# The delta stage's products with the inverses as 32x32 tiles in crossed row groups, its key products as tiles of 32 columns

## The reference, cut to what matters

```python
q = l2norm(silu(h @ Wq)); k = l2norm(silu(h @ Wk)); v = silu(h @ Wv)
beta = sigmoid(h @ Wb); alpha = exp(-exp(A_log) * softplus(h @ Wa + dt_bias))
def step(S, (q_t, k_t, v_t, a_t, b_t)):
    S = S * a_t
    delta = (v_t - k_t @ S) * b_t
    S = S + outer(k_t, delta)
    return S, q_t @ S * scale
o = rms_norm(o) * o_norm_w * silu(h @ Wg); out = o @ Wo
```

## Time and profile before

| | |
|---|---|
| Time, median of 3 runs | 2097.25 us (2090.12 to 2099.79) |
| The profiled execution | 2083.64 us, span 2081.6 us |
| PE busy | 1736.5 us (83%) |
| DVE, ACT, POOL busy | 1258.1, 1067.8, 873.5 us |
| Rows ahead of the loop | from about 1063 to 1148 us |
| 24 looped rows | 1148 to 1765 us, most 25.28 us apart |
| 8 rows of the tail | 1765 to 1975 us, most 26.3 to 26.5 us apart |

### The profile page before, as it was taken

The page is one execution under the profiler, slowest core; times in us unless marked ns, Lnnn a source line. Parts: engine busy times, 40 slices in busy tenths (PEclk is TensorE's granted clock), DMA queues, the critical chain, the costliest instruction groups (busy, mean ns, idle before and its releaser), DMA issues. The chain is left out here.

```text
span 2081.6 us, 37284 instructions
## 1 busy us (share of the span) xinstructions
PE 1736.5 (83%) x12051; PEld 1241.9 (60%) x12051; DVE 1258.1 (60%) x3243; ACT 1067.8 (51%) x3158; POOL 873.5 (42%) x1095
## 2 busy tenths in 40 slices
PE   0899629974299849999868999999999999899887
PEld 0344429864198826556557677777777777555533
DVE  7587624536345378787667566655665665456556
ACT  0443204331143328788544566656666666666643
POOL 0246646546555513343318756070606060622233
PEclk9997659995599959999979999999999999999999
DMA  2920023322122250000023221212121212110001
GB/s 63 416 69 22 30 72 107 97 85 84 49 70 63 58 195 23 26 25 25 25 77 80 60 57 47 57 47 57 47 58 46 57 48 60 53 48 29 25 12 41
DMA packets 155838, 135.89 MB, mean 65 GB/s; under 512 B 87957, under 2 KB 128214, under 8 KB 153494
## 3 DMA queue, kind: packets, MB, share of 16 engines
q1 hardware_dynamic: 146582, 115.08, 18.9%
q0 software_dynamic: 9088, 18.70, 2.8%
HBM read 77.17 MB, written 56.54 MB: 64 GB/s over the span
## 5 line engine op out<-in xcount | busy, mean ns | idle before, releaser
L2676 DVE TENSOR_TENSOR delta_sv<-delta_sv,delta_zp 32x256 f32<-32x256 f32 x384 | 161.2, 420 | 168.4 <-PE delta_zp L2317 162.0
L818 POOL DMA_INDIRECT y<-moe_y,moe_aim x156 | 177.1, 1135 | 161.4 <-DVE moe_y L958 69.0
L2589 POOL TENSOR_TENSOR delta_dd<-delta_ll,delta_minus 128x1024 f32<-128x1024 f32 (+1 forms) x9 | 24.3, 2700 | 382.4 <-DMA delta_ll<-lanes 382.3
L1771 ACT ACTIVATE field_p<-field_sp,field_nm 128x128 f32<-128x128 f32 x512 | 179.9, 408 | 0.9 <-DVE field_nm L1855 0.8
L2596 POOL TENSOR_TENSOR delta_dd<-delta_dd,delta_prod 128x30 f32<-128x30 f32 (+11 forms) x270 | 151.4, 561 | 21.1
L2594 POOL TENSOR_TENSOR delta_prod<-delta_ll,delta_dd 128x30 f32<-128x30 f32 (+11 forms) x270 | 139.4, 516 | 21.2
L2317 PE MATMUL delta_zp<-delta_sv,delta_ct 128*32 128x128 f32 x1536 | 122.5, 281 | 20.1 <-DVE delta_sv L2676 12.4
L2285 PE MATMUL delta_xp<-delta_la,delta_di 128*128 128x256 f32 x512 | 121.4, 392 | 12.9 <-DMA delta_di<-inverses 7.0
L1771 ACT ACTIVATION_READ_ACCUMULATOR field_p<-field_sp,field_nm 128x1 f32 x512 | 127.6, 249 | 0.0
L2317 PEld LDWEIGHTS delta_zp<-delta_sv,delta_ct 128*32 128x32 f32 x1536 | 70.3, 110 | 85.0 <-DVE delta_sv L2676 50.7
L2285 PEld LDWEIGHTS delta_xp<-delta_la,delta_di 128*128 128x128 f32 x512 | 97.3, 194 | 37.6 <-issue 25.3
(11 more groups left out here) (564 smaller groups left out, 4554.3 us busy)
## 6 DMA issues: line engine op xcount, KB each, us to landing
delta_al<-alpha SPq DMA_DIRECT2D x33, 512.0 KB, 4.4
pairs<-c_none SPq DMA_DIRECT2D x16, 1032.0 KB, 16.3
moe_xg<-pairs SPq DMA_DIRECT2D x78, 129.0 KB, 2.2
moe_yt<-y SPq DMA_DIRECT2D x16, 512.0 KB, 4.5
w_E<-in_E_dram SPq DMA_DIRECT2D x1, 4624.0 KB, 36.9
w_E<-in_E_dram SPq DMA_DIRECT2D x8, 578.0 KB, 4.0
lanes<-delta_la SPq DMA_DIRECT2D x128, 32.0 KB, 1.7
delta_di<-inverses SPq DMA_DIRECT2D x64, 64.0 KB, 2.3
```

The source lines that it names most:

```text
L818: nc.gpsimd.indirect_dma_start(results, bass.IndirectOffsetOnAxis(ap=aim[:, t % AR, j:j + 1], axis=0), y[:, t % YS, j, :], None).then_inc( ...
L1771: last = nc.scalar.activation(p[:, slot, h, :], s_ps[i][:, k, :], ACT.Exp, bias=nm[:, slot, h:h + 1], accum_out=zs[:, slot, h:h + 1])
L2676: nc.vector.tensor_tensor(sv[rows, two, :], sv[rows, two, :], z_ps[2 * pair // HH][rows, at, :], ALU.subtract).then_inc(s["z_kept"], 1)
```

## The change

The pairs of heads get numbers, 0 to 3, and CROSS = [0, 3, 1, 2]. For pair c the tokens' blocks of la lie crossed: block g of the keys is written to the 32 partitions g ^ CROSS[c] (^ is exclusive or) instead of g. What is per token on the partitions of la is crossed with it: eye, ball_at (a crossed copy of beta), and ck, for which a third product with headpick is made from a crossed copy of the norms' first 128 columns (four copies of 32 partitions each). squares for kn stay uncrossed.

key_products makes, for each head, four products with 32 columns of keys as weights, each over the tokens from its own block on (256, 192, 128 or 64 columns); the very first row's are over all 256. invert makes four products for each head: weights are a 32x32 inverse, read from the 32 partitions g ^ CROSS, written to the partitions g of x_ps, over the columns behind block g only. di shrinks to 32 columns and is not cleared any more. store_lanes issues 16 DMAs a row, one for each partition group and pair of heads. PE's wait for the placed inverses moves ahead of norms of the row before, and its wait for sq at the start of a looped step goes. In norms the two heads of a partition group are now 2g and 2g + 1.

```diff
+    CROSS, STORED = [0, 3, 1, 2], 16 * NB * PAIRS
+    def crossed(ap, pair):
+        part = CROSS[pair]
+        return bass.AP(ap.tensor, ap.offset + BL * part, [list(ap.ap[0]), [-2 * BL if part & 2 else 2 * BL, 2], [-BL if part & 1 else BL, 2], [1, BL]])
+    def by_blocks(ap):
+        return ap.rearrange("p (a b c) -> p a b c", a=2, b=2)
+    PRODUCTS = [(j + c, g ^ 3 * (j // 2)) for c in range(2) for g in (0, 1) for j in (0, 2)] + [(j + c, g ^ 3 * (j // 2)) for c in range(2) for g in (3, 2) for j in (0, 2)]
+    def lanes_of(part):
+        return slice(part * BL, (part + 1) * BL)
...
+        ball_at = m.sb("ball_at", [128, GROUPS + 1, GB * H])
...
-        di = m.sb("di", [128, 2, GB * H, T])
+        di = m.sb("di", [128, 2, GB * H, BL])
...
                 def store_lanes(p):
                     sp.wait_ge(s["la_kept"], p.n * 2 + 2)
-                    for g in range(NB):
-                        sp.dma_start(dram["lanes"][p.pair, g, p.b * H:(p.b + 1) * H, :, :].rearrange("h j i -> j h i"),
-                                     la[g * BL:(g + 1) * BL, p.slot, :, g * BL:(g + 1) * BL]).then_inc(lanes_out[p.half], 16)
+                    for part in range(NB):
+                        for pair in range(PAIRS):
+                            at, two = p.b * H + 2 * pair, slice(2 * pair, 2 * pair + 2)
+                            sp.dma_start(dram["lanes"][p.pair, part, at:at + 2, :, :].rearrange("h j i -> j h i"),
+                                         la[lanes_of(part), p.slot, two, lanes_of(part ^ CROSS[pair])]).then_inc(lanes_out[p.half], 16)
...
-                        sp.dma_start(di[g * BL:(g + 1) * BL, pair, two, g * BL:(g + 1) * BL],
+                        sp.dma_start(di[lanes_of(g), pair, two, :],
...
                         for g in range(4):
-                            last = nc.tensor.matmul(k_rows[g * 32:(g + 1) * 32, :], w["headrow"][:, a, :], sq[:, g + 4 * a, :],
+                            last = nc.tensor.matmul(k_rows[g * 32:(g + 1) * 32, :], w["headrow"][:, a, :], sq[:, 2 * g + a, :],
                                                     start=(a == 0), stop=(a == 1))
...
                     nc.tensor.matmul(k_cols, nrow[:, 0:T], w["headpick"][:], start=True, stop=True)
-                    nc.tensor.matmul(q_cols, nrow[:, T:], w["headpick"][:], start=True, stop=True).then_inc(s["ncol_made"], 1)
-
-                def key_products(p, i):
-                    for j, h in enumerate(range(i * HH, (i + 1) * HH)):
-                        last = nc.tensor.matmul(x_ps[i][:, j, :], kq[:, p.half, h, 0:T], kq[:, p.half, h, :], start=True, stop=True)
+                    nc.tensor.matmul(k_at, nrow[:, 2 * T:], w["headpick"][:], start=True, stop=True)
+                    nc.tensor.matmul(q_cols, nrow[:, T:2 * T], w["headpick"][:], start=True, stop=True).then_inc(s["ncol_made"], 1)
+                def key_products(p, i, whole=False):
+                    by_kind = lambda ap: ap.rearrange("p (a t) -> p a t", t=T)
+                    for j, g in PRODUCTS:
+                        h, first = i * HH + j, 0 if whole else g * BL
+                        last = nc.tensor.matmul(by_kind(x_ps[i][lanes_of(g ^ CROSS[h // 2]), j, :])[:, :, first:], kq[:, p.half, h, lanes_of(g)],
+                                                by_kind(kq[:, p.half, h, :])[:, :, first:], start=True, stop=True)
                     last.then_inc(s["kkq_made"], 1)
                 def invert(r, i):
-                    for j, h in enumerate(range(i * HH, (i + 1) * HH)):
-                        last = nc.tensor.matmul(x_ps[i][:, j, :], di[:, r.pair, r.b * H + h, :], la[:, r.slot, h, :], start=True, stop=True)
+                    for j in (0, 2, 1, 3):
+                        h = i * HH + j
+                        for g in range(NB):
+                            rows, first = lanes_of(g ^ CROSS[h // 2]), (g + 1) * BL
+                            last = nc.tensor.matmul(x_ps[i][lanes_of(g), j, first:], di[rows, r.pair, r.b * H + h, :], la[rows, r.slot, h, first:],
+                                                    start=True, stop=True)
                     last.then_inc(s["ca_made"], 1)
...
                 def step(t, k):
                     r, q, p, before, g = Row(t, k), Row(t, k + AHEAD), Row(t, k + AHEAD + 1), Row(t, k - 1), group_of(t, k)
-                    if r.b % 2 == 0:
-                        pe.wait_ge(inv_in[r.b // 2][r.pair], (t + 1) * 16 * NB)
+                    if not looped(t) and k and r.b % 2 == 0:
+                        inverses_placed(r, t)
                     for i in range(2):
-                        if looped(t) or k == 0:
-
-                            pe.wait_ge(s["sq_kept"], r.n + AHEAD + 1)
-                        else:
+                        if not looped(t) and k:
                             pe.wait_ge(s["ad_kept"], (r.n - 1) * 2 + i + 1)
...
                     if looped(t):
+                        if k % 2:
+                            inverses_placed(Row(t, k + 1), t + (k + 1) // RING)
                         norms(p)
...
-                nc.gpsimd.memset(di[:], 0.0)
...
-                    ch.link(nc.vector.tensor_scalar(bt[:], ball[:].rearrange("p g h -> p (g h)")[:, bass.ds(p.n * H, H)], 0.0, None, ALU.add))
+                    ch.link(nc.vector.tensor_scalar(bt[:], ball_at[:].rearrange("p g h -> p (g h)")[:, bass.ds(p.n * H, H)], 0.0, None, ALU.add))
                     dve.wait_ge(s["n_made"], p.n + 1)
-                    nc.vector.tensor_copy(nrow[:], k_rows).then_inc(s["nrow_kept"], 1)
+                    nc.vector.tensor_copy(nrow[:, 0:2 * T], k_rows)
+                    for pair in range(PAIRS):
+                        rows = lanes_of(pair)
+                        last = nc.vector.tensor_copy(by_blocks(nrow[rows, 2 * T:]), crossed(k_rows[rows, 0:T], pair))
+                    last.then_inc(s["nrow_kept"], 1)
                 def keep_columns(p, squares, eps_q):
                     dve.wait_ge(s["ncol_made"], p.n + 1)
-                    ch.link(nc.vector.tensor_scalar(squares, k_cols, EPS, None, ALU.add))
+                    ch.link(nc.vector.tensor_scalar(ck[:], k_at, EPS, None, ALU.add))
+                    nc.vector.tensor_scalar(squares, k_cols, EPS, None, ALU.add)
                     nc.vector.tensor_scalar(eps_q, q_cols, EPS, EPS * T, ALU.add, ALU.mult)
-                    ch.link(nc.vector.reciprocal(ck[:], squares))
+                    ch.link(nc.vector.reciprocal(ck[:], ck[:]))
                     nc.vector.tensor_tensor(ck[:], ck[:], bt[:], ALU.mult).then_inc(s["ck_made"], 1)
...
-                ch.link(nc.vector.tensor_copy(eye[:], w["ident"][:].unsqueeze(1).to_broadcast([128, H, T])))
+                for h in range(H):
+                    last = nc.vector.tensor_copy(by_blocks(eye[:, h, :]), crossed(w["ident"][:], h // 2))
+                ch.link(last)
...
+                by_head = lambda ap: ap.rearrange("p g (b h) -> p (g b) h", h=H)
+                for pair in range(PAIRS):
+                    two = slice(2 * pair, 2 * pair + 2)
+                    for part in range(NB):
+                        last = nc.vector.tensor_copy(by_head(ball_at[lanes_of(part), :, :])[:, :, two],
+                                                     by_head(ball[lanes_of(part ^ CROSS[pair]), :, :])[:, :, two])
+                ch.link(last)
...
-    a["headpick"] = ((quarter == heads % 4) & (place == heads // 4)).astype(f)
+    a["headpick"] = ((quarter == heads // 2) & (place == heads % 2)).astype(f)
```

13 lines of the change are left out of this document (8 added, 5 removed).

## The result

The changed kernel takes **2140.18 us** (median of 4 runs, 2132.11 to 2149.16) against 2095.31 us for the kernel before (4 runs, 2090.12 to 2099.79): ratio 1.022, 95% interval 1.020 to 1.024. It is slower by 2.2%; the forecast was 2077 us, range 2062 to 2115. The profiled execution took 2143.29 us, span 2141.4, 59.8 us more than the span of before.

The account below looks back on a forecast made before the run. In looped rows TensorE's and VectorE's chains, ending almost together, were taken as the bound. Ahead +8.3, loop -16.8, tail -11.8 us sum to -20.3: profiled 2083.64 to 2063, given as 2077 by the median's 13.6 us offset; range 2062 to 2115.

Parts of the forecast that it names:

- rival 5: Looped rows: PE's new idle ahead of headpick, among narrow tiles, drops the clock to 1.2 GHz; +14 us, 2111; chance 0.06.
- new 1.6 us idle of PE ahead of headpick: Looped row: PE stands idle from about 10.8 until nrow is released at 12.26, as the copies delay nrow.
- The key products: Looped row: 32 narrower products take 2.3 us instead of 3.45 us of starts; from 3.0 us the row stops gaining.
- Rival 1: Key products: column groups work two at a time, both halves take 4.4 us; +33 us, 2130, slower; chance 0.10.
- Rival 3: PE can't be fed small records; at 45 ns each both kinds of product take 2.9 us; +3 us, 2100; chance 0.14.
- rival 2: Key products start strictly in order, one whose group is taken holding all behind it; +64 us, 2161; chance 0.04.
- Ahead of the loop: Rows before the loop: 16 stores delay alpha and the first inverses, so the loop starts +8.3 us later.
- The copies: DVE's four added 32x128 copies out of PSUM, for the crossed norms: 0.29 us each, 1.16 us a row.
- The products with the inverses: 32 small-tile products take 1.7 us instead of 3.45, with bounds of 1.5 and 3.0 us.
- The tail: Eight tail rows, without key products or copies, gain 1.48 us each by shorter products with the inverses: -11.8 us.
- rival 4: Row groups don't overlap: products with the inverses take 3.0 us, tail earns 0.4 us a row; -12 us, 2085; chance 0.08.
- rival 6: Copies are cheap and SP issues the stores fast: 2060; chance 0.06.

Follow-up runs that it names:

- e2: Changed kernel with every product with an inverse given twice in a row, filling TensorE's wait for nrow; 2120.5 us, ratio to before 1.011.
- e3: Changed kernel with the crossed row of norms made by TensorE in norms instead of by four VectorE copies; 2096.5 us, ratio to before 1.000.
- e5: Kernel of e3 with the key products of a half visiting all four column groups before coming back to the first; 2080.0 us, ratio to before 0.991.
- e7: Kernel before, with only the lanes' stores changed: 16 DMAs of two heads per row instead of 4 of eight; 2111.5 us, ratio 1.007.
- e4: Changed kernel with alpha for row k+2 issued ahead of row k's 16 stores, ahead of the loop; 2139.5 us, ratio to before 1.020.
- e9: Changed kernel with both hk and alpha issued ahead of the 16 stores of lanes, ahead of the loop; 2128.1 us, ratio to before 1.016.

## Why the prediction was wrong

**The step that failed first is the clock.** The prediction had it as rival 5, with a chance of 0.06 and 1.4 us a row. The mechanism is right, and so nearly is the size (26.8 against 25.2 us in a row with a fall), but the sum put it at nothing and the chance was far off. What I set against it, the tail's wait of 1.59 us at a clock of 1.00, is shorter and has whole 128x128 products on both sides; which of the two makes the difference isn't shown. The change puts 2 us of idle into each row, right behind products on 32x32 tiles. e2 and e3 take the idle away in two ways, and in both the clock stays up but at the loop's turns. e2's loop is 22.9 us shorter with plain rows as in the changed kernel (25.2 us), so that is the clock. e3's is 43.1 us shorter, and its plain rows are 1.0 us shorter too (24.2 us). The forecast's own "new 1.6 us idle of PE ahead of headpick" was the sign.

**The key products** were taken as 2.3 us with 3.0 us as the point at which the looped row stops gaining; they are 3.06. That is the term that was mis-sized, and it takes the loop's gain away even at full clock: the gate starts 9.20 us after the first product with an inverse, where the forecast had 8.48. Of these 0.72 us the key products make 0.54 (they start 2.99 us ahead of the gate, forecast 2.45), the later nrow 0.18. Rival 1 (two column groups at a time) named the right cause and priced it too high, 4.4 us: it let nothing overlap across a change of groups. The starts of single records in the trace show that groups 3 and 2 begin while groups 0 and 1 are in their second round, so eight rounds of some 0.58 us take five steps. e5's order takes 2.46 us, near my 2.3. Rival 3 (records can't be fed faster than one in 45 ns) falls with it: 2.46 us over 64 records is 38 ns.

**The Trainium skill's rule** of strict order ("TensorE: Matmul & The Clock Gate", Part 3) was rival 2. The single records of the key products contradict it for column groups: in the changed kernel a product of 192 columns on group 1 starts 14 ns after that of 256 columns on group 0, ahead of the second product of group 0, which is given before it and starts 0.44 us later. What holds is order within a group, and a limit on how far ahead others are taken.

**Ahead of the loop** the forecast was +8.3 us, the result +20.7. The stores' pitch was near (7.4 to 8.8 us for 16, forecast 7.2), and so were the waits for alpha (1.62, 0.15, 2.85 and 1.72 us for "1 to 2.3"). The step that failed is the list of what is queued behind them: alpha, but not hk, although the prediction names hk as queued there in the loop. e7 gives the stores alone 17.3 us, e4 shows that alpha without hk is worth nothing, e9 takes 8.3 us back with both; what it leaves, 12.4 us, is nearer to the 8.3 us of the forecast, which had no hk wait in it. The clock is low for longer there too, 24.6 us of the stretch against 10.8 (16.3 in e9).

**What held.** The copies are 0.285 us each against 0.29. The products with the inverses take 1.6 us against 1.7. The wait at headpick is 2.04 us against 1.6 (and the forecast's own terms, 12.26 less 10.8, give 1.5); nrow comes 0.2 us later than summed. The 216 ns between records of the products with the inverses are right, though the working shown for them, 3.34 us over 15, gives 223: in the single starts the first distance is 321 ns, all others 216, and the 0.1 us more stands where the forecast puts its 0.1 us for a change of tile shape. SyncE's 16 stores don't delay di in the loop (e7, +1.6 us). The last four intervals of the tail are 24.5 to 25.3 us, forecast about 25. The tail is -5.7 us instead of -10.4, since only these four gain (99.5 us against 106.0); the first three take 78.7 against 77.9, and all of the tail's falls lie in them (13.7 us at half clock, before 10.2). Row groups overlap (rival 4 falls), and cheap copies (rival 6) didn't come.

**The sum again, from the runs:** ahead +20.7, of it 17.3 by the stores. In the loop +31.8: about 23 by the clock (e2). The rest, 8.9, is what e2 has over before. It lies at the loop's turns, since e2's plain rows are those of before: there the falls are longer (10.2 and 13.7 us in e2, one of 3.4 before), and TensorE waits for its own next instructions twice instead of once. No run takes these waits away. One turn, before and in the changed kernel:

```profile
1354.99 5.40 PE L2285 MATMUL delta_xp<-delta_la,delta_di 128*128 128x256 f32 x16 [2.73 <-issue]
```

```profile
1396.57 1.95 PE L2311 MATMUL delta_xp<-delta_la,delta_di 32*32 32x224 f32 x46 [2.67 <-issue]
...
1400.10 1.06 PE L2311 MATMUL delta_xp<-delta_la,delta_di 32*32 32x128 f32 x18 [1.58 <-issue]
```

In the tail -5.7.

## What to carry to other kernels

Work that leaves an engine's path leaves a gap, and on TensorE a gap that comes back in every row can cost twice, by itself and by the clock behind it. Take away what it waits for, or fill it; here a permutation done by TensorE's reading of its operand instead of four copies turned +2.2% into 0, and another order of products and of loads brought it to -1.2 to -1.5%. Give narrow column tiles to all four groups in turn; and when a queue gets longer, list every transfer behind it for every stretch, not only the one that comes to mind.
